# Shorter GpSimd sums, a later place for c's second half, and another order in the first and last pair of a two-layer gated network kernel

## The chip, the cores and the metric

One core of one Trainium2 chip. The metric is the device time of one execution in microseconds, as the median of several runs. TensorE is called PE in the profile, VectorE DVE, ScalarE ACT, GpSimd POOL and SyncE SP; PEld is TensorE's weight load, which overlaps the matmuls.

## The reference, cut to what matters

```python
x = x + L0_ffn(L0_cond(x, slot), ...)      # conditioned: x @ W + b + 2 (x @ A[slot]) @ B[slot]
x = x + L1_ffn(L1_cond(x, lang), ...)      # both linear, each with routed adapters (top 2 of 8)

# L0_ffn: y = (silu(c @ Wg.T) * (c @ Wu.T)) @ Wd.T            512 -> 1376 -> 512
# L1_cond: c = x @ W.T + 2 * sum_e gate[e] * (x @ A[e]) @ B[e]
# L1_ffn: y = c @ W2.T + b + 2 * sum_e combine[e] * (c @ A2[e]) @ B2[e]
```

x has 128 x 32 = 4096 tokens of 512 features, all in float32. The gates of the second layer are a softmax over the two best of eight experts.

## The kernel before, in words

**Tiles.** The tokens lie along the columns: 8 tiles of 512 tokens (NT = 8), each of four blocks of 128 features (KC = 4), 128 x 512 elements a block. Two tiles form a pair, a *stage* s of the middle part and a pair u of the last part (NS = 4).

**Precision.** Every float32 operand is split in two: `hi`, a copy rounded to TensorE's float32r made by ScalarE, and `lo`, the difference, made by VectorE. Three matmuls (hi hi, hi lo, lo hi) stand for one product; `mm3`, which calls `mm` at L1813, issues them. So behind each operand stand a ScalarE instruction, a VectorE instruction and a TensorE wait for the second.

**Seven products.** The large products are done on 2 x 2 blocks with seven block products instead of eight (numbered 1 to 7, order `ORDER = [1, 7, 6, 2, 5, 4, 3]`). They need sums of the operands: t1 to t4 of the token side, s1 to s4 of the weight side. Four banks (a, y, w, z) take the products; ScalarE copies a bank into the next one where two results share a product (`begin_y`, `begin_z`), and VectorE adds the seventh product, kept in a scratch tile, to two of them (`sum_c21`, `sum_c22`, and v).

**Order of the program.** First the conditioning layer for 8 tiles, whose result c is stored to memory. Then, for each of the four stages: gate and up products (slots "g", 11 blocks of 128 hidden columns with seven products each), with `silu` on ScalarE and the products h on VectorE (L1481, L1488), and the down products (slots "d", 35 steps). Weights come through a ring of 12 tiles that SyncE fills in the order in which TensorE uses them; its other transfers stand in that same queue (`extras`). Last comes a stage of folded weights (the two linear layers of L1 are multiplied together, `weight_product`, five of them) and four pairs u = 0 to 3, each of two blocks (mp = 0, 1), with routers.

**Around the change.** Each engine runs its own program in order; semaphores tie them. Nothing is scheduled at run time, so the place of a call in `act_program`, `dve_program` or `pe_program` is its place in the queue.

- *Pair sums* (`pair_sums`, L834 to L855): GpSimd forms t3, t1, t2 and t4 of a stage's result, four operations on 128 x 1024 elements, and counts them in `pair_sum_done`. For stages 0 to 2 they run in the next stage's second gate block; SyncE stores them (`store_sums`) behind weight loads. For stage 3 they run at the start of the last stage, and ScalarE's `route_x(0)` and `copy_7_l` wait for them. The four sums over the folded weights (L922 to L928) follow on GpSimd.
- *c's operands* (`COP_BEHIND`, L520): during the down steps of stage s the fourteen operands of c for stage s + 1 are split, each behind a chosen down step n. The first seven are of c's first half, the other seven of its second. `cop_begin` forms two differences on VectorE when c has landed; `load_c(s + 1, 1)` on SyncE waits for the seventh split. `op_split` and `op_rest` are the ScalarE and VectorE halves of down operand n; a down operand needs the place of operand n - 8, so TensorE's slot of that one. `down_z22` (the v of the down product, L1498) runs behind n = 32, and TensorE's `down_single(s, 0)` waits for it.
- *Weight products*: `weight_product(i)` on TensorE fills a right and a left bank; ScalarE copies them, VectorE makes the low parts (L1567 right, L1570 left) and so frees them. `route_x(0)` on TensorE, four groups c of 12 matmuls, takes for its first group the right bank of product 3, then the left one of 3, then right and left of 4.
- *A pair of the last stage*: the programs at L1311 to L1365 (ScalarE), L1770 to L1807 (VectorE) and L2094 to L2128 (TensorE). `router(i, t)` is a chain of 11 to 14 small VectorE operations for tile t (i = 0: first adapter, i = 1: second) with one exponential on ScalarE in it. `turn_h(i, t)` transposes the routed tile on TensorE, copies it on ScalarE and makes its low part on VectorE (L1647), which the products `out_h1` and `out_h2` need. `route_h(t)` feeds the first adapter's result to the second router. `split_t(u, i)` splits a stored sum t_i (L1529). In a block, TensorE's product 7 waits for `gc22_done` of the block before (VectorE, `sum_c22_l`, L1546) and for the split of t3:

```python
if i == 7:
    ...
        e.wait_ge(gc22_done, gate_turn(n - 1))
...
    t = {7: 3, 6: 2, 5: 1, 4: 4}[i]
    e.wait_ge(t_lo_done, t_split(u, t))
```

  Products 4 and 5 wait for `yz_done`, ScalarE's `begin_z_l` (L1271), which is behind product 6 of the block.

## Time and profile before

| | |
|---|---|
| median of 3 runs | 1000.36 us (999.42 to 1001.5) |
| the profiled execution | 1001.15 us |
| its span in the profile | 999.4 us |
| mean granted TensorE clock | 0.998 |
| instructions | 13989 |

The span runs from the first to the last instruction of the profile; the time of the same execution is 1.75 us longer. In the rows of a group, the names are written output <- inputs, the shape is partitions x elements, "idle before" is the time for which the engine did nothing ahead of the instructions, and the arrow names what ended it. A timeline row gives the start and the duration in us; several like instructions in a row are merged (x2). Matmuls are pipelined: their durations overlap, and one of 512 columns starts 0.227 us after the other.

### The profile page before, as it was taken

How to read it: one execution, taken by the hardware profiler on the slowest of the kernel's cores; microseconds unless marked ns; L12 is line 12 of the kernel's file. 1: busy time of each engine (PE TensorE's matmuls, PEld its weight loads, DVE VectorE, ACT ScalarE, POOL GpSimd, SP SyncE). 2: the span in 40 equal slices, each digit the busy share in tenths (PEclk: the TensorE clock that was granted, in tenths of full speed). 3: DMA queues.
4: the chain of work that ended last, by engine and by line, in shares of the span. 5: the costliest groups of instructions: out<-in, count | busy, mean ns of one | idle time of the engine just before them, and what ended most of it. 6: DMA issues, size and time to landing. Idle time of an engine off the chain costs nothing.

```text
span 999.4 us, 13989 instructions
## 1 busy us (share of the span) xinstructions
PE 983.9 (98%) x4787; PEld 829.5 (83%) x4787; DVE 599.5 (60%) x969; ACT 464.5 (46%) x854; POOL 244.6 (24%) x192
## 2 busy tenths in 40 slices
PE   8999999999999999999999999999999998999998
PEld 7888888888878788888888887888888988888876
DVE  5644596776983632685533497342376587585762
ACT  5635566555742333571333373333356363535342
POOL 5232332654300621400513220341141520000000
PEclk9999999999999999999999999999999999999999
DMA  8997866676968876877887767986687730615122
GB/s 282 358 324 287 307 220 245 216 267 234 336 230 293 269 208 191 281 243 252 276 265 193 239 225 251 324 274 198 191 307 281 261 122 22 232 45 209 66 104 85
DMA packets 121485, 230.11 MB, mean 230 GB/s; under 512 B 12612, under 2 KB 12612, under 8 KB 121160
## 3 DMA queue, kind: packets, MB, share of 16 engines
q1 hardware_dynamic: 118880, 220.81, 65.9%
q0 software_dynamic: 2400, 8.41, 2.3%
q8 instruction: 39, 0.64, 0.3%
q14 instruction: 30, 0.25, 0.1%
q10 hardware_dynamic: 136, 0.01, 0.0%
HBM read 165.74 MB, written 63.44 MB: 229 GB/s over the span
## 4 chain that ended last, share of the span: by engine, by line
PE 79%; DVE 14%; issue 2%; DMA 2%; ACT 1%; SPq 0%; DVEq 0%; ACTq 0%
PE bank L1813 78%; DVE op_lo L1452 5%; DVE cop_lo L1438 2%; DMA c<-c_scratch 2%; PE bank L1837 1%; DVE h_lo L1457 1%; ACT xs_hi L1120 1%; PE bank L1974 1%; DVE h L1488 1%; DVE s L1488 1%; DVE xs_lo L1523 0%; DMA slot_i<-in_slots 0%; DVE c L1432 0%; DVE c L1443 0%; DVE c_t L1430 0%
## 5 line engine op out<-in xcount | busy, mean ns | idle before, releaser
L1813 PE MATMUL bank<-cop_hi,wring 128*128 128x512 f32 x1234 | 381.1, 389 | 0.7 <-DVE v L1466 0.7
L1813 PEld LDWEIGHTS bank<-cop_hi,wring 128*128 128x128 f32 x1234 | 231.6, 188 | 50.0 <-DVE v L1466 1.6
L1813 PE MATMUL bank<-cop_lo,wring 128*128 128x512 f32 x616 | 239.7, 389 | 0.0
L1813 PE MATMUL bank<-op_hi,wring 128*128 128x512 f32 x560 | 174.6, 390 | 1.9 <-DVE op_lo L1452 1.9
L1466 DVE TENSOR_TENSOR v<-bank,p7s 128x512 f32<-128x512 f32 x44 | 30.4, 691 | 191.1 <-PE bank L1813 191.0
L1813 PEld LDWEIGHTS bank<-cop_lo,wring 128*128 128x128 f32 x616 | 115.6, 188 | 23.7
L1813 PEld LDWEIGHTS bank<-op_hi,wring 128*128 128x128 f32 x560 | 105.1, 188 | 25.1 <-issue 3.1
L1813 PE MATMUL bank<-op_lo,wring 128*128 128x512 f32 x280 | 109.0, 389 | 0.0
L1066 ACT ACTIVATE s<-bank 128x512 f32<-128x512 f32 x44 | 26.3, 598 | 117.9 <-PE bank L1813 117.8
L1452 DVE TENSOR_TENSOR op_lo<-h,op_hi 128x512 fp32r<-128x512 f32 x100 | 77.7, 794 | 3.8 <-ACT op_hi L1023 3.6
L1023 ACT ACTIVATE op_hi<-h 128x512 fp32r<-128x512 f32 x100 | 62.3, 626 | 13.4 <-PE bank L1813 12.6
L820 POOL TENSOR_TENSOR h_t<-h,h 128x512 f32<-128x512 f32 x20 | 26.6, 1328 | 170.3 <-DVE h L1488 170.3
L1035 ACT ACTIVATE bank<-bank 128x512 f32<-128x512 f32 x44 | 25.6, 582 | 77.5 <-PE bank L1813 77.5
L1813 PEld LDWEIGHTS bank<-op_lo,wring 128*128 128x128 f32 x280 | 52.6, 188 | 10.8
L1813 PE MATMUL bank<-xa_hi,w_hi 128*128 128x512 f32 x128 | 50.8, 397 | 1.2 <-DVE w_lo L1383 1.2
L850 POOL TENSOR_TENSOR t_sum<-x_second,x_second 128x1024 f32<-128x1024 f32 x3 | 7.2, 2401 | 179.8 <-DMA x_second<-x_scratch 179.8
L1813 PE MATMUL bank<-xa_lo,w_hi 128*128 128x512 f32 x128 | 50.0, 391 | 0.0
L1813 PE MATMUL bank<-xa_hi,w_lo 128*128 128x512 f32 x128 | 49.9, 390 | 0.0
L1471 DVE TENSOR_TENSOR p7s<-bank,p7s 128x512 f32<-128x512 f32 x44 | 30.4, 691 | 23.9 <-PE bank L1813 23.7
L1057 ACT ACTIVATE s<-bank 128x512 f32<-128x512 f32 x44 | 26.3, 598 | 30.6 <-PE bank L1813 30.6
L1042 ACT ACTIVATE p7s<-bank 128x512 f32<-128x512 f32 x44 | 26.3, 598 | 30.4 <-PE bank L1813 30.4
L1488 DVE TENSOR_TENSOR h<-s,v 128x512 f32<-128x512 f32 x40 | 34.9, 874 | 8.2 <-ACT s L1066 8.0
(228 smaller groups left out, 1916.1 us busy)
## 6 DMA issues: line engine op xcount, KB each, us to landing
wring<-wgu_scratch SPq DMA_DIRECT2D x231, 256.0 KB, 2.9
wring<-wd_scratch SPq DMA_DIRECT2D x140, 256.0 KB, 5.3
wgu_scratch<-wring SPq DMA_DIRECT2D x77, 256.0 KB, 3.6
x_raw<-in_x SPq DMA_DIRECT2D x32, 256.0 KB, 7.5
c_scratch<-c_out SPq DMA_DIRECT2D x32, 256.0 KB, 2.8
c<-c_scratch SPq DMA_DIRECT2D x32, 256.0 KB, 4.4
xs_raw<-x_scratch SPq DMA_DIRECT2D x16, 512.0 KB, 6.9
out<-res SPq DMA_DIRECT2D x32, 256.0 KB, 2.1
```

The source lines that it names most:

```text
L820: e.tensor_tensor(h_t3[p][:, :], h22[p][:, :], h12[p][:, :], ALU.subtract).then_inc(t3_done, 1)
L1023: e.activation(op_hi[n % N_OP][:, :], op_source[i][p][:, :], ACT.Copy).then_inc(op_hi_done, 1)
L1035: e.activation(bank_y[b][:, :], bank_a[b][:, :], ACT.Copy).then_inc(ay_done, 1)
L1042: e.activation(p7s[b][:, :], bank_w[b][:, :], ACT.Copy).then_inc(p7s_done, 1)
L1057: e.activation(s1[j % 2][:, :], bank_a[j % 2][:, :], ACT.Silu).then_inc(silu1_done, 1)
L1066: e.activation(s2[j % 2][:, :], bank_z[j % 2][:, :], ACT.Silu).then_inc(silu2_done, 1)
L1438: e.tensor_tensor(cop_lo[i][:, q, :], cop_source[i][:, :], plain(cop_hi[i][:, q, :]), ALU.subtract).then_inc(cop_lo_done, 1)
L1452: e.tensor_tensor(op_lo[n % N_OP][:, :], op_source[i][p][:, :], plain(op_hi[n % N_OP][:, :]), ALU.subtract).then_inc(op_lo_done, 1)
L1466: e.tensor_tensor(v[b][:, :], bank_z[b][:, :], p7s[b][:, :], ALU.add).then_inc(gc22_done, 1)
L1471: e.tensor_tensor(p7s[b][:, :], bank_y[b][:, :], p7s[b][:, :], ALU.add).then_inc(gc21_done, 1)
L1488: e.tensor_tensor(dst[:, :], s2[b][:, :], v[b][:, :], ALU.mult).then_inc(h2_done, 1)
L1813: return e.matmul(out_ap, lhs, rhs, start=start, stop=stop, skip_group_check=True)
```

## The change

It does four things. `PIECES = 4`: each of the four pair sums is made in four operations of 128 x 256 elements (two halves k, two column ranges h) instead of one of 128 x 1024, each counts in `pair_sum_done`, and all waits for that semaphore are multiplied; each of the four waits for all pieces of the one before (t2 had no such wait before). The four sums over the folded weights are made in two operations each, of 128 x 256. In `COP_BEHIND` the eighth operand of c (the first of its second half) stands behind down step 27 instead of 25, and the following ones move up so that the thirteenth stands behind step 32, called behind `down_z22`, instead of step 31. `weight_product(3)` is called before `split_t(0, 3)`, on ScalarE and VectorE. And in the pairs: the first pair's `router(0, 2)` comes behind the sums of the first block instead of before the transposed tiles; of the router tiles' copies on ScalarE one instead of two stands before an exponential; in the third pair (u = 2, the last that prepares another) `split_t(3, 3)` and `split_t(3, 2)` come before `router(1, 6)`, and `turn_h(0, 7)` behind the block's sums.

```diff
--- before.py
+++ after.py
@@ -467,6 +467,7 @@
         return 4 * u + t_order(u).index(i) + 1
 
     S_SPLITS = [3, 1, 2, 4]
+    PIECES = 4
 
     def l_place(u, i):
 
@@ -517,7 +518,7 @@
         return rhs2_sb[:, i, :], rhs2_hi[:, i, :], rhs2_lo[:, i, :]
 
 
-    COP_BEHIND = dict(zip((11, 13, 14, 15, 16, 19, 20, 25, 27, 28, 29, 30, 31, 33), range(len(cop_order))))
+    COP_BEHIND = dict(zip((11, 13, 14, 15, 16, 19, 20, 27, 28, 29, 30, 31, 32, 33), range(len(cop_order))))
 
 
 
@@ -605,7 +606,7 @@
                     else:
                         e.wait_ge(x2_stored["c11", mp], DMA * s)
                         e.wait_ge(x2_stored["c21", mp], DMA * s)
-                        e.wait_ge(pair_sum_done, 4 * s)
+                        e.wait_ge(pair_sum_done, PIECES * 4 * s)
                     e.dma_start(res[mp][:, :], x[2 * s, mp]).then_inc(res_in[mp], DMA)
                     e.dma_start(res[2 + mp][:, :], x[2 * s, 2 + mp]).then_inc(res_in[2 + mp], DMA)
             if pos == slot_at["d", 1, 1] and s == NS - 1:
@@ -657,7 +658,7 @@
 
         def store_sums(s):
             for n, (i, tile) in enumerate(((3, t3_sum), (1, x2_second[0]), (2, t2_sum), (4, x2_second[1]))):
-                e.wait_ge(pair_sum_done, 4 * s + n + 1)
+                e.wait_ge(pair_sum_done, PIECES * (4 * s + n + 1))
                 e.dma_start(t_dram[s, i - 1].rearrange("k p f -> p k f"), tile[:, :, :]).then_inc(t_stored, DMA)
 
         def load_x2(u, j, h):
@@ -670,7 +671,7 @@
                 e.wait_ge(pe_slot, NS * N_SLOT)
                 for mp in range(2):
                     e.wait_ge(x2_stored["c12", mp], DMA * NS)
-                e.wait_ge(pair_sum_done, 4 * NS - 2)
+                e.wait_ge(pair_sum_done, PIECES * (4 * NS - 2))
             else:
                 e.wait_ge(pe_acc, l_mark(u - 2, 1, {(0, 0): 1, (0, 1): 5, (1, 0): 5, (1, 1): 3}[j, h]))
             e.dma_start(xs_raw[u % 2][j][:, 2 * h:2 * h + 2, :],
@@ -847,12 +848,17 @@
                 e.wait_ge(cop_lo_done, 14 * NS)
             else:
                 e.wait_ge(x2_second_in, 2 * DMA * (s + 1))
-            e.tensor_tensor(t3_sum[:, :, :], b22[:, :, :], b12[:, :, :], ALU.subtract).then_inc(pair_sum_done, 1)
-            e.wait_ge(pair_sum_done, n + 1)
-            e.tensor_tensor(t1[:, :, :], b12[:, :, :], b11[:, :, :], ALU.subtract).then_inc(pair_sum_done, 1)
-            e.tensor_tensor(t2_sum[:, :, :], t3_sum[:, :, :], b11[:, :, :], ALU.add).then_inc(pair_sum_done, 1)
-            e.wait_ge(pair_sum_done, n + 3)
-            e.tensor_tensor(t4[:, :, :], b21[:, :, :], t2_sum[:, :, :], ALU.subtract).then_inc(pair_sum_done, 1)
+
+            for done, (out_, in0, in1, op) in enumerate((
+                    (t3_sum, b22, b12, ALU.subtract), (t1, b12, b11, ALU.subtract),
+                    (t2_sum, t3_sum, b11, ALU.add), (t4, b21, t2_sum, ALU.subtract))):
+                if done > 0:
+                    e.wait_ge(pair_sum_done, PIECES * (n + done))
+                for k in range(2):
+                    for h in range(PIECES // 2):
+                        cols = slice(h * 2 * TOK // PIECES, (h + 1) * 2 * TOK // PIECES)
+                        e.tensor_tensor(out_[:, k, cols], in0[:, k, cols], in1[:, k, cols],
+                                        op).then_inc(pair_sum_done, 1)
 
         e.iota(part_i[:, :], [[0, 1]], base=0, channel_multiplier=1).then_inc(pool_const, 1)
         e.memset(ident[:, :], 0.0).then_inc(pool_const, 1)
@@ -918,14 +924,14 @@
         pair_sums(NS - 1)
         a11, a21 = m2_raw[:, 0:2, 0:2 * P], m2_raw[:, 0:2, 2 * P:]
         a12, a22 = m2_raw[:, 2:4, 0:2 * P], m2_raw[:, 2:4, 2 * P:]
-        e.wait_ge(m2_raw_done, 4)
-        e.tensor_tensor(s_raw[3][:, :, :], a11, a21, ALU.subtract).then_inc(s_sum_done, 1)
-        e.wait_ge(m2_raw_done, 2 * KC)
-        e.tensor_tensor(s_raw[1][:, :, :], a21, a22, ALU.add).then_inc(s_sum_done, 1)
-        e.wait_ge(s_sum_done, 2)
-        e.tensor_tensor(s_raw[2][:, :, :], s_raw[1][:, :, :], a11, ALU.subtract).then_inc(s_sum_done, 1)
-        e.wait_ge(s_sum_done, 3)
-        e.tensor_tensor(s_raw[4][:, :, :], a12, s_raw[2][:, :, :], ALU.subtract).then_inc(s_sum_done, 1)
+        for done, (i, in0, in1, op) in enumerate((
+                (3, a11, a21, ALU.subtract), (1, a21, a22, ALU.add), (2, s_raw[1], a11, ALU.subtract),
+                (4, a12, s_raw[2], ALU.subtract))):
+            e.wait_ge(m2_raw_done, 4 if i == 3 else 2 * KC)
+            if done > 1:
+                e.wait_ge(s_sum_done, 2 * done)
+            for k in range(2):
+                e.tensor_tensor(s_raw[i][:, k, :], in0[:, k, :], in1[:, k, :], op).then_inc(s_sum_done, 1)
 
 
 
@@ -1125,13 +1131,13 @@
             e.activation(hi, first, ACT.Copy).then_inc(t_hi_done, 1)
 
         def split_s(i):
-            e.wait_ge(s_sum_done, S_SPLITS.index(i) + 1)
+            e.wait_ge(s_sum_done, 2 * (S_SPLITS.index(i) + 1))
             e.wait_ge(pe_ring, ring_full("left", KC, 0))
             e.activation(s_hi[i][:, :, :], s_raw[i][:, :, :], ACT.Copy).then_inc(fold_hi_done, 1)
 
         def route_x(t, cs=range(TC)):
             if t == 0:
-                e.wait_ge(pair_sum_done, 4 * NS)
+                e.wait_ge(pair_sum_done, PIECES * 4 * NS)
                 for mp in range(2):
                     e.wait_ge(x2_stored["c12", mp], DMA * NS)
                     e.wait_ge(x2_stored["c22", mp], DMA * NS)
@@ -1252,7 +1258,7 @@
             n = l_turn(u, mp)
             e.wait_ge(pe_acc, l_mark(u, mp, 7))
             if n == 0:
-                e.wait_ge(pair_sum_done, 4 * NS)
+                e.wait_ge(pair_sum_done, PIECES * 4 * NS)
                 for half in range(2):
                     e.wait_ge(x2_stored["c11", half], DMA * NS)
                     e.wait_ge(x2_stored["c21", half], DMA * NS)
@@ -1294,8 +1300,8 @@
         split_x2(0, 1, 0)
         weight_product(2)
         split_x2(0, 1, 1)
+        weight_product(3)
         split_t(0, 3)
-        weight_product(3)
         split_t(0, 2)
         weight_product(4)
         split_t(0, 4)
@@ -1334,17 +1340,17 @@
                 route_x(a + 2, (0, 1))
                 router(1, a if u == 0 else b)
                 route_x(a + 2, (2, 3))
-                route_x(b + 2, (0, 1))
+                route_x(b + 2, (0,))
                 router(*((1, b) if u == 0 else (0, a + 2)))
-                route_x(b + 2, (2, 3))
-                if u == 0:
-                    router(0, a + 2)
+                route_x(b + 2, (1, 2, 3))
             else:
                 router(1, b)
             turn_h(1, a)
             turn_h(1, b)
             close_l(u, 0, "c11")
             close_l(u, 0, "c12")
+            if u == 0:
+                router(0, a + 2)
             begin_y_l(u, 1)
             copy_7_l(u, 1)
             if more:
@@ -1747,8 +1753,8 @@
         split_x2(0, 1, 0)
         weight_product(2)
         split_x2(0, 1, 1)
+        weight_product(3)
         split_t(0, 3)
-        weight_product(3)
         split_t(0, 2)
         weight_product(4)
         split_t(0, 4)
@@ -1779,29 +1785,30 @@
                 split_x2(u + 1, 1, 0)
                 split_x2(u + 1, 1, 1)
             router(1, b)
-            if more:
+            if more and u > 0:
                 router(0, a + 2)
             turn_h(1, a)
             turn_h(1, b)
             sum_c21_l(u, 0)
             sum_c22_l(u, 0)
             if more:
+                if u == 0:
+                    router(0, a + 2)
                 router(0, b + 2)
                 turn_h(0, a + 2)
                 route_h(a + 2)
+                split_t(u + 1, 3)
+                split_t(u + 1, 2)
                 if u + 2 < NS:
-                    split_t(u + 1, 3)
-                    split_t(u + 1, 2)
                     split_t(u + 1, 1)
+                    turn_h(0, b + 2)
                 else:
                     router(1, a + 2)
-                turn_h(0, b + 2)
             sum_c21_l(u, 1)
             sum_c22_l(u, 1)
             if more:
                 if u + 2 == NS:
-                    split_t(u + 1, 3)
-                    split_t(u + 1, 2)
+                    turn_h(0, b + 2)
                     split_t(u + 1, 1)
                 split_t(u + 1, 4)
                 route_h(b + 2)
```

## Rows read from the trace of the kernel before

**Rows 1.** The page, part 1: busy time and share of each engine.

```profile
PE 983.9 (98%) x4787; PEld 829.5 (83%) x4787; DVE 599.5 (60%) x969; ACT 464.5 (46%) x854; POOL 244.6 (24%) x192
```

**Rows 2.** TensorE's waits: who waited <- whom, us in total, times, longest.

```profile
PE bank L1813 <- DVE hg_lo L1647: 3.3, 1, 3.3
PE bank L1813 <- DVE op_lo L1452: 1.9, 3, 0.9
PE bank L1813 <- issue: 1.8, 1, 1.8
...
PE bank L1813 <- DVE m_lo L1567: 0.8, 1, 0.8
PE bank L1813 <- DVE v L1466: 0.7, 2, 0.5
PE bank L1813 <- DVE v L1498: 0.6, 3, 0.2
```

**Rows 3.** Timeline, VectorE and GpSimd, 320 to 336: start, us, instruction, [idle before].

```profile
326.23 2.90 DVE L1481 TENSOR_TENSOR h<-s,p7s 128x512 f32<-128x512 f32 x1
...
328.55 2.84 POOL L853 TENSOR_TENSOR t_sum<-t_sum,res 128x1024 f32<-128x1024 f32 x1
```

**Rows 4.** GpSimd's groups: by line (busy, mean ns), and min/median/max ns.

```profile
L850 POOL TENSOR_TENSOR t_sum<-x_second,x_second 128x1024 f32<-128x1024 f32 x3 | 7.2, 2401 | 179.8 <-DMA x_second<-x_scratch 179.8
...
L791 POOL TENSOR_TENSOR gs<-wg_raw,wu_raw x11: 736/740/1245, 121.6 to 230.6; 128x256 f32<-128x256 f32 x11
```

**Rows 5.** Timeline of SyncE's queue, 336 to 342: the fourth store of sums.

```profile
339.77 1.27 SPq L661 DMA_DIRECT2D t_scratch<-x_second  x1
```

**Rows 6.** Timeline, TensorE 287 to 290 and VectorE 280 to 300.

```profile
288.00 0.39 PE L1813 MATMUL bank<-op_hi,wring 128*128 128x512 f32 x1
289.30 0.47 PE L1813 MATMUL bank<-op_hi,wring 128*128 128x512 f32 x1 [0.92 <-DVE op_lo L1452]
...
285.74 0.69 DVE L1430 TENSOR_TENSOR c_t<-c,c 128x512 f32<-128x512 f32 x1 [4.24 <-DMA c<-c_scratch]
...
296.49 1.28 DVE L1498 TENSOR_TENSOR v<-bank,v 128x512 f32<-128x512 f32 x2
```

**Rows 7.** Timeline of VectorE, 799 to 806, at the folded weights.

```profile
799.79 2.30 DVE L1529 TENSOR_TENSOR t_lo<-t_raw,t_hi 128x1024 fp32r<-128x1024 f32 x1
...
803.09 0.28 DVE L1567 TENSOR_TENSOR m_lo<-bank,m_hi 128x128 fp32r<-128x128 f32 x1
```

**Rows 8.** Last stage, first and second pair: timeline; last row a window with PEclk.

```profile
842.26 0.19 DVE L1584 SCALAR_TENSOR_TENSOR logit<-lang_hot,lx 128x32 f32<-128x32 f32 x1
846.44 1.29 DVE L1647 TENSOR_TENSOR hg_lo<-bank,hg_hi 128x512 fp32r<-128x512 f32 x2
...
843.38 0.60 PE L1974 MATMUL bank<-ident,hg 128*128 128x128 f32 x4
...
851.61 0.48 PE L1813 MATMUL bank<-xs_hi,m_hi 128*128 128x512 f32 x1
...
894.80 0.60 PE L1974 MATMUL bank<-ident,hg 128*128 128x128 f32 x4
...
898.30 0.40 PE L1813 MATMUL bank<-xs_hi,m_hi 128*128 128x512 f32 x1
...
898.86 0.19 DVE L1595 TENSOR_TENSOR diff<-logit,top 128x32 f32<-128x32 f32 x1
...
856.00 0.58 ACT L1271 ACTIVATE bank<-bank 128x512 f32<-128x512 f32 x1 [0.55 <-PE bank L1813]
...
849.00:850.00 1.00, 1.00 (x4) 0.76 (x3) 0.69 (x1) 0.00 (x0) 0.00 (x0) 0.50 0.18 70
```

**Rows 9.** Timeline of VectorE, 956 to 968, at the last pair.

```profile
957.89 0.19 DVE L1591 TENSOR_REDUCE top<-lx 128x4 f32<-128x32 f32 x1
...
962.94 0.69 DVE L1647 TENSOR_TENSOR hg_lo<-bank,hg_hi 128x512 fp32r<-128x512 f32 x1
...
964.75 2.35 DVE L1529 TENSOR_TENSOR t_lo<-t_raw,t_hi 128x1024 fp32r<-128x1024 f32 x2
```

## The prediction

> **What bounds the kernel now.** I read the page first, then TensorE's waits, then the timeline around each wait. The page shows TensorE busy for 98% of the span [rows 1], so the matmuls are the bound, and an edit on another engine pays only where TensorE waits. The list of TensorE's waits [rows 2] is the whole purse: 3.3 us for one half of a transposed adapter tile, 1.9 in three waits for `op_lo`, 1.8 that it calls "issue", 0.8 for a half of the folded weights, 0.7 in two waits for v of the gate and 0.6 in three for v of the down product. The idle time understates a gap, since a matmul is drawn 0.39 long while they start every 0.227 us: between the two matmuls of [rows 6] lie 1.30 us, so the `op_lo` gap of 0.92 cost 1.07, and the first matmul after it ran 0.08 long (0.47 against 0.39). I add 0.25 us to each listed wait.
>
> **Pair sums in pieces, stages 0 to 2.** The product h of VectorE, both inputs in SBUF, takes 2.90 us while GpSimd adds [rows 3], against 0.69 for such an operation undisturbed [rows 6]. The next two VectorE operations have the same length, and behind them waits v, which TensorE wants. The row of GpSimd beside it, 2.84 against 2.40 undisturbed [rows 4], shows that the engines take turns by whole instructions, also where GpSimd's next instruction has no semaphore wait ahead of it (L852 to L853). A piece of 256 columns takes 0.74 [rows 4]. So each of the three VectorE operations waits at most 0.74 instead of 2.2; VectorE gains over 4 us, and v is late by only 0.5 and 0.2. Both waits go: 0.7 + 2 x 0.25 = **1.2 us**. The price: sixteen pieces are 11.8 us against 4 x 2.4 = 9.6, and with three or four VectorE turns of 0.6 to 0.7 they end about 14 us after their start at 323.7, near 338. SyncE issues the fourth store at 339.8 [rows 5], and its queue of weight loads runs twelve slots ahead of TensorE, so its wait for the count 16 holds nothing up. Bounds: 0.7 to 1.3.
> By the Trainium skill's "GPSIMD Engine Reference", section 3.1, 2048 elements take 4497 ns, which would make a piece 0.56 us and the cut free. By that the sums would end 2.8 us sooner and nothing in the forecast would change, as the fourth store has the time either way; the row of 0.74 says otherwise and is what I use.
>
> **Second half of c two operands later.** VectorE waits for c from step 25, until 285.74 [rows 6]; `op_lo` 26 stands behind the wait, and TensorE stops. After the change steps 26 and 27 are split before it: their ScalarE halves need TensorE slots 18 and 19, which end near 278.7 and 280.1 (slots of 6 x 0.227 = 1.36 us, counted back from 288.2), so they are done by 282. Next due is `op_lo` 28, at 288.2 + 2 x 1.36 = 290.9: c's two differences, one split, one difference and the split of 28 are five operations of 0.6 to 0.7 from 285.74, ready at 289.2. Step 29: ready 291.3, due 292.3. The second wait of the stage is for v of the down product, ready at 297.8 [rows 6]. Three operations of 0.6 (splits 26 and 27, and c's twelfth split, which now comes after v) leave the queue before it: 296.0, due 288.2 + 4 x 1.36 + 2.72 = 296.4. All six waits of three stages go: 1.9 + 0.6 + 6 x 0.25 = 4.0, measured start to start 3.9; I take **3.9**. The slack of 0.4 for v is thin, so the bounds are 2.4 and 4.0. No DMA is moved: c's load is gated by the seventh split of the first half, whose place is unchanged.
>
> **Folded weights (start of the last stage).** VectorE's split of t takes 2.30 us (1.15 of it waiting for GpSimd) ahead of the fourth weight product, whose half is free at 803.4 [rows 7]; TensorE has then been idle for 0.8, since 802.6. Now the weight product goes first: it starts at about 799.8 instead of 802.0, and its half is free near 801.2. That wait of 0.8 + 0.25 goes. But two splits of t now stand together ahead of the fifth weight product: fourth done 802.0, then ScalarE and VectorE for the two splits, 2.7, and 0.2: 804.9 undisturbed, with GpSimd's pieces in between (0.3 and 0.7) 805.9. TensorE wants that bank at 802.5 + 3.0 = 805.5. I expect a new wait of about 0.3 there: net **0.8**, bounds -0.3 and 1.05. The sums over the folded weights are earlier by the fourth product's two us; they have no waiter now. GpSimd's pair sums end near 800 instead of 798.8, and their first waiter, ScalarE's copy of the router tiles, has until about 807.
>
> **First pair of the last stage.** VectorE runs a router, 842.26 to 846.44, ahead of the adapter tile that TensorE wants, and ScalarE has the router's exponential ahead of the same tile. Afterwards TensorE ran at a granted clock of 0.50 [rows 8], 1.2 GHz. From the transposes to the next block's first matmul pass 851.61 - 843.38 = 8.23 us; in the second pair, where no router stands there, 898.30 - 894.80 = 3.50. With the router behind the block's sums both pairs have the same order: **4.7 us**, slow clock included. What is late next: two routers now follow the sums. By the second pair's row the first one's difference ends 0.75 us after the block starts [rows 8], the second's 4.18 later, at 4.93; ScalarE's exponential stands before the copy that starts bank z (exponential 0.14 to the next start, copy 0.58), so the copy ends at 5.7. TensorE wants it after four products, 4 x 1.36 = 5.44. So a new wait of 0.3, with its start 0.4: net **4.3**, bounds 3.3 and 4.75. The moved copies of router tiles (one ahead of an exponential, not two) let the second router run about 1 us earlier, which nobody waits for.
>
> **Last pair.** The "issue" wait is for product 7, which needs two things: the split of t3, done at 965.9 (the first half of the row of 964.75), and the previous block's v sum, done at 964.8, because it gives bank w free. Today the order is router (957.89 to 962.94), tile, two sums, splits [rows 9]. The change puts two splits first (2.26 us from 957.8), then the router (5.05), then the sums (0.6 + 0.68): the splits are ready at 960.1, but the v sum only at 957.8 + 2.26 + 5.05 + 1.28 = 966.4. Product 7 then starts 0.5 later than today. ScalarE's exponential comes 2.3 later with the router, and the tile copies queued behind it delay TensorE by less than that, ahead of the same wait. **-0.5 us**, bounds -0.8 and 0.
>
> **Sum.** 1.2 + 3.9 + 0.8 + 4.3 - 0.5 = 9.7 us. The profiled execution took 1001.15 us for a span of 999.4 (1.75 around it), so it would take 991.4. It is 0.8 above the median of the runs, 1000.36: **990.7 us** there. About 0.2%, 2 us, is what a measurement of this kernel can tell from no change.
>
> **Rivals.**
> (a) The last pair pays: if the split were the only thing product 7 waits for, the 1.8 + 0.25 would go instead of 0.5 coming: 988.1. For it: the release came 0.1 after the split and 1.2 after the sum. Against it: the program's wait for the sum. 6%.
> (b) GpSimd keeps the port through pieces that have no semaphore wait between them. Four pieces then block VectorE as one instruction did, 3.0 us: the 1.2 and the 0.8 are lost, 992.7. Against it: VectorE got its turn between L852 and L853. The rule behind it is the Trainium skill's "SBUF — State Buffer", section "Who interferes with whom", by which issue order decides who blocks. 6%.
> (c) The thin slacks break: c lands later than 285.5 after its issue, or the two routers in a row delay the second pair's tiles too. Half of 3.9 and 2 us more are lost: 994.6. Against it: VectorE is busy for only 60% of the span [rows 1], and its work in that block has not grown. 9%.
> (d) Slower: each piece pays for the port. The pair sums of the last stage start at 786.55 and ScalarE's router copies wait for them; TensorE needs the first by 808.5. At p us a piece, TensorE stops for 16p - 21.5, and the waits of the first and third terms stay (2.0). It is slower than before from 16p = 29.2, p = 1.8. At 2.4, the longest piece of [rows 4], 1.245, plus a VectorE split of 1.15 every time, it would be 990.7 + 2.0 + 16.9 = 1009.6. The longest of the eleven speaks for it, their median of 0.74 and VectorE's few operations in that stretch against. 2%.
> (e) The edits change nothing at c's operands, because c is the limit whatever stands behind it: 994.6 as well. 4%, since the operations behind the wait are named.
> The forecast has the remaining 73%, its own range 989.2 to 992.6. The range over all, 988.3 to 994.0, takes in (a), (b) and the bounds of the terms; it leaves out (d), most of (c) and (e). Faster by over 0.2%: 95%, all but (d) and a sum of lower bounds; within: 3%; slower: 2%.
>
> **What would show it.** In TensorE's waits: no `op_lo`, no v of either kind, no `hg_lo` of 3.3, no slow clock near 845; short new ones behind a copy to bank z in the first pair (0.1 to 0.3 idle), and behind `m_lo` (0 to 0.5); a wait of about 1.9 in the last pair, now released by the sum of L1546's line. VectorE's h product beside the sums at 1.4 or less, GpSimd's pieces at 0.74. A saving under 6 us, or a last pair without a wait, would prove a step wrong.

## The result, and the profile after

The kernel before was run beside each set, on the same chip.

| | time, us (median) | ratio to before |
|---|---|---|
| before, beside the first set | 999.89 | |
| after, first set | 994.2 (992.9 to 994.35) | 0.9939, 95% [0.9922, 0.9957] |
| before, beside the second set | 1001.21 | |
| after, second set | 992.97 (991.5 to 993.54) | 0.9923, [0.9908, 0.9938] |
| forecast | 990.7 (988.3 to 994.0) | |

It is faster, as forecast, by 5.7 us in the first set and 8.2 in the second instead of 9.7, and the first median lies 0.2 above the range. The profiled execution took 994.31 us for a span of 992.6.

The page of after, part 1:

```profile
PE 982.7 (99%) x4787; PEld 830.4 (84%) x4787; DVE 586.8 (59%) x969; ACT 464.9 (47%) x854; POOL 256.0 (26%) x244
```

GpSimd is busy for 11.4 us more [rows 1]. VectorE is busy for 12.7 less, since the time for which an operation is blocked counts as busy and it no longer stands behind whole sums in stages 0 to 2. TensorE's waits of after:

```profile
PE bank L1820 <- DVE res L1552: 1.9, 1, 1.9
PE bank L1820 <- DVE warm L1663: 1.5, 1, 1.5
PE bank L1820 <- ACT bank L1041: 0.9, 1, 0.9
PE bank L1820 <- DVE w_lo L1389: 0.8, 1, 0.8
PE bank L1820 <- issue: 0.8, 1, 0.8
PE bank L1820 <- ACT res L1285: 0.3, 2, 0.2
PE bank L1820 <- ACT bank L1277: 0.2, 1, 0.2
```

Of the waits of before [rows 2] that the sum counted, `hg_lo` (3.3), `op_lo`, both v and `m_lo` are gone. The 1.9 for `res` and the 0.2 for ScalarE's bank were foretold; the 0.8 called "issue" was not, and it stands elsewhere than the old one. The timelines of VectorE and GpSimd beside the pair sums:

```profile
327.20 0.94 DVE L1487 TENSOR_TENSOR h<-s,p7s 128x512 f32<-128x512 f32 x1
328.06 1.22 DVE L1458 TENSOR_TENSOR op_lo<-h,op_hi 128x512 fp32r<-128x512 f32 x1
329.21 1.22 DVE L1494 TENSOR_TENSOR h<-s,v 128x512 f32<-128x512 f32 x1
...
324.76 2.83 POOL L860 TENSOR_TENSOR t_sum<-x_second,x_second 128x256 f32<-128x256 f32 x4 [59.18 <-DMA x_second<-x_scratch]
327.67 4.05 POOL L860 TENSOR_TENSOR x_second<-x_second,res 128x256 f32<-128x256 f32 x4
```

The three VectorE operations take 0.94 to 1.22 instead of 2.9 [rows 3]; the second sum takes 4.05 in four pieces, because VectorE has its turns between them. The last stage of after, timelines of TensorE, VectorE, GpSimd and ScalarE:

```profile
820.01 0.47 PE L1820 MATMUL bank<-xs_hi,s_hi 128*128 128x512 f32 x1 [0.78 <-issue]
...
806.83 0.72 DVE L1590 SCALAR_TENSOR_TENSOR logit<-lang_hot,lx 128x32 f32<-128x32 f32 x1
...
810.51 0.19 DVE L1630 SCALAR_TENSOR_TENSOR picked<-rank,expo 128x32 f32<-128x32 f32 x1 [0.32 <-ACT expo L1156]
...
818.68 1.23 DVE L1535 TENSOR_TENSOR xs_lo<-xs_raw,xs_hi 128x1024 fp32r<-128x1024 f32 x1
...
806.50 1.70 POOL L934 TENSOR_TENSOR s_raw<-m_raw,s_raw 128x256 f32<-128x256 f32 x2
...
808.23 0.63 ACT L1136 ACTIVATE s_hi<-s_raw 128x512 fp32r<-128x512 f32 x1 [1.21 <-POOL s_raw L934]
810.18 0.23 ACT L1156 ACTIVATE expo<-diff 128x32 f32<-128x32 f32 x1
...
849.15 0.58 ACT L1277 ACTIVATE bank<-bank 128x512 f32<-128x512 f32 x1
849.78 0.50 PE L1820 MATMUL bank<-xs_hi,s_hi 128*128 128x512 f32 x1 [0.17 <-ACT bank L1277]
...
958.46 0.68 DVE L1552 TENSOR_TENSOR res<-bank,res 128x512 f32<-128x512 f32 x1
959.19 0.50 PE L1820 MATMUL bank<-t_hi,s_hi 128*128 128x512 f32 x1 [1.93 <-DVE res L1552]
```

Read from below: product 7 of the last pair starts 0.05 after the v sum, which now comes behind splits and router. Product 5 of the first pair's second block waits for ScalarE's copy, whose predecessor is an exponential. And product 5 of the very first block waits until 820.01 for VectorE's low half of t1 (its tile bears the name `xs_lo`), done at 819.91. VectorE is late because two routers stand ahead of that split, and the first of them is late. Its exponential (810.18) stands on ScalarE behind the split of s4, which waits for GpSimd's last sum over the folded weights (ends at 808.20).

The exponential is only one of two ways in which these sums reach VectorE. Before, the same router began its chain of small operations 5.4 us ahead of the first block, and the first of them took 0.18:

```profile
810.28 0.18 DVE L1584 SCALAR_TENSOR_TENSOR logit<-lang_hot,lx 128x32 f32<-128x32 f32 x1
...
812.59 0.23 ACT L1150 ACTIVATE expo<-diff 128x32 f32<-128x32 f32 x1
```

After, it begins 4.9 ahead of the block; that first operation takes 0.72 beside GpSimd's running pieces, and the chain up to the use of the exponential 0.8 more than before. Then VectorE stands idle for 0.32 until the exponential is there. Of the 1.5 us by which this router ends later against the block, 0.5 are the later start, 0.8 the slower operations and 0.2 the exponential. By an estimate from the same rows, the exponential alone would have held the router up for nearly as long, since it starts 1.6 ahead of the block instead of 3.1.

Where the 6.8 us between the spans are, start to start between the same matmuls in both traces:

| stretch | before | after | difference | forecast |
|---|---|---|---|---|
| start of the span to the first gate block | 147.63 | 149.09 | +1.5 | 0 |
| stages 0 to 3 | 637.09 | 632.72 | -4.4 | -5.1 |
| folded weights to the first h1 product | 55.46 | 55.44 | 0.0 | -0.8 |
| to the first pair's second block | 11.43 | 6.77 | -4.7 | -4.7 |
| to the last pair | 93.30 | 93.62 | +0.3 | +0.4 |
| the last pair and the end | 54.51 | 54.95 | +0.4 | +0.5 |

Two of the losses lie outside what the change touches. Timelines of TensorE after, in the opening and in stage 0:

```profile
7.12 0.63 PE L1820 MATMUL bank<-xa_lo,w_hi 128*128 128x512 f32 x1
7.55 0.63 PE L1820 MATMUL bank<-xa_hi,w_lo 128*128 128x512 f32 x1
...
210.48 0.50 PE L1820 MATMUL bank<-cop_hi,wring 128*128 128x512 f32 x1 [0.87 <-ACT bank L1041]
```

The first matmuls start 0.43 apart, not 0.227, for some 3.5 us (1.7 lost); the wait at 210 cost 1.03. Without it stages 0 to 3 gained 5.4.

### The profile page after: what moved, and what is told of

Its sections match the earlier page's. It is cut to its first block, busy times and chain, and to the rows that moved or that the text cites. A ratio compares the mean times of both kernels' runs of the same rounds, so it can differ in the third digit from the quotient of the medians.

```text
span 992.6 us, 14042 instructions
## 1 busy us (share of the span) xinstructions
PE 982.7 (99%) x4787; PEld 830.4 (84%) x4787; DVE 586.8 (59%) x969; ACT 464.9 (47%) x854; POOL 256.0 (26%) x244
## 4 chain that ended last, share of the span: by engine, by line
PE 96%; DVE 1%; ACT 1%; issue 1%; DMA 0%; SPq 0%; ACTq 0%; DVEq 0%
PE bank L1820 95%; PE bank L1844 1%; PE bank L1981 1%; DMA w_raw<-in_w 0%; ACT xs_hi L1126 0%; ACT bank L1277 0%; DVE hg L1644 0%; DVE t_lo L1535 0%; DVE greater L1624 0%; ACT res L1285 0%; DVE diff L1601 0%; DVE top L1597 0%; DVE wins L1620 0%; DVE rank L1627 0%; DVE greater L1618 0%
## 5 line engine op out<-in xcount | busy, mean ns | idle before, releaser
L1458 DVE TENSOR_TENSOR op_lo<-h,op_hi 128x512 fp32r<-128x512 f32 x100 | 72.9, 747 | 3.3 <-ACT op_hi L1029 3.1
L1029 ACT ACTIVATE op_hi<-h 128x512 fp32r<-128x512 f32 x100 | 62.7, 627 | 13.6 <-PE bank L1820 12.7
L860 POOL TENSOR_TENSOR t_sum<-x_second,x_second 128x256 f32<-128x256 f32 x12 | 8.9, 780 | 177.3 <-DMA x_second<-x_scratch 177.3
L776 POOL DMA_INDIRECT ab<-in_ab_table,row_i x16 | 18.7, 1171 | 81.9 <-DVE b_lo L1400 75.8
```

The costliest lines, as they stand in the source:

```text
L776: e.indirect_dma_start(out=ab[g][:, :], out_offset=None, in_=ab_table, in_offset=bass.IndirectOffsetOnAxis(ap=row_i[:, col:col + 1], axis= ...
L1029: e.activation(op_hi[n % N_OP][:, :], op_source[i][p][:, :], ACT.Copy).then_inc(op_hi_done, 1)
L1458: e.tensor_tensor(op_lo[n % N_OP][:, :], op_source[i][p][:, :], plain(op_hi[n % N_OP][:, :]), ALU.subtract).then_inc(op_lo_done, 1)
```

## Experiments

Each is the changed kernel with the edit shown, unless it says otherwise. Traces are compared start to start, since the 95% intervals of the medians are +/- 1.2 us at best and 2.4 at worst. "Theory A" and "theory B" are those of the expectation that stands with the run.

**1. The changed kernel again.** 

> The changed kernel once more. Theory A (the parts gave what the walk through the queues says, about 9.0 us, and the missing 2.6 us of the profiled execution are chance delays in code that the change leaves alone: a granted clock of 0.5 in the first 4 us and one late load of gate weights near 210): the profile has neither or only one of the two, its span is 990 to 991.5, and the waits from 240 on are the same to 0.2 us. Theory B (the change itself slows the opening, by its place in memory or by its longer programs): both delays stand there again at the same size, span 992.6.

992.97 us, ratio 0.9923; in its trace the wait at 210 is gone and the opening takes 6.1 instead of 7.3; span 990.2, 9.2 below before. All waits from 240 on are the same. So the two losses were chance, and the change is worth 8 us by this set (7.7 by the ratio).

**2. c's operands as before.**

```diff
-    COP_BEHIND = dict(zip((11, ..., 20, 27, 28, 29, 30, 31, 32, 33), ...
+    COP_BEHIND = dict(zip((11, ..., 20, 25, 27, 28, 29, 30, 31, 33), ...
```

> Only the place of c's second half is put back to step 25. Theory A: the waits for op_lo and for the v of the down product come back in stages 0 to 2, 3.9 us start to start, so 3.9 us slower than the changed kernel. Theory B (c's landing was the limit either way): the time of the changed kernel within 1 us.

996.09 us, 0.9952 [0.9937, 0.9966]: 3.1 slower than run 1. Its waits on TensorE, and when VectorE got c in the first and third stage:

```profile
PE bank L1820 <- DVE op_lo L1458: 0.5, 1, 0.5
...
PE bank L1820 <- DVE v L1504: 0.2, 1, 0.2
...
285.38 0.69 DVE L1436 TENSOR_TENSOR c_t<-c,c 128x512 f32<-128x512 f32 x1 [2.58 <-DMA c<-c_scratch]
602.13 0.69 DVE L1436 TENSOR_TENSOR c_t<-c,c 128x512 f32<-128x512 f32 x1 [3.81 <-DMA c<-c_scratch]
```

Only the third stage waits. From the first of c's DMA issues to VectorE's start pass 5.6, 5.5 and 6.8 us in the three stages, against 7.2, 6.5 and 7.1 in the execution that the forecast was worked out from. The lost time follows c's landing, and that execution had three late ones. Over the 14 traces it runs from 5.5 to 7.5.

Start to start, this trace loses 1.2 us to the undone edit (1.0 of it at the two waits), not 3.1. Of the rest of its 3.8 against run 1's, 1.1 lie in the opening and 1.6 behind a fall of the granted clock in the last pair. So the trace bears out theory A's mechanism, and its 3.9 only for an execution in which c lands late.

**3. The first pair's router back ahead of the tiles** (ScalarE and VectorE).

```diff
-            if more and u > 0:
+            if more:
                 router(0, a + 2)
```

> Only the router's place in the first pair is put back (the copies of the router tiles stay as changed). Theory A: TensorE's wait of about 3 us in front of out_h2 comes back with the slow clock behind it, and the new wait of 0.3 for the copy to bank z goes: 4.2 us slower than the changed kernel. Theory B (the slow clock would have come anyway or costs nothing): 3 us or less.

997.11 us, 0.9957 [0.9943, 0.9971], 4.1 slower than run 1. TensorE's wait, and a window behind it (busy times, then PEclk, DMA share, GB/s):

```profile
PE bank L1818 <- DVE hg_lo L1653: 2.3, 1, 2.3
...
845.00:847.00 2.00, 2.00 (x8) 1.57 (x8) 1.24 (x2) 0.00 (x0) 0.00 (x0) 0.75 0.35 132
```

The stretch to the second block is 10.56 against 6.77, so 3.8 us longer; the wait at bank z is gone (0.4), which makes 3.4 net against the 4.2 of theory A, and the granted clock falls again. The old wait was a microsecond longer [rows 2]. Here the router starts 2.1 us ahead of the transposes instead of 1.1; the moved copies of router tiles, still in place, may be why, which no run separates.

**4. The third pair's order as before** (splits behind the sums, the tile ahead).

```diff
                 route_h(a + 2)
-                split_t(u + 1, 3)
-                split_t(u + 1, 2)
...
+                    split_t(u + 1, 3)
+                    split_t(u + 1, 2)
                     split_t(u + 1, 1)
```

> Only the third pair's order is put back. Theory A (product 7 is released by the sum of v in the changed kernel, 0.4 to 0.5 later than by the split in the order before): 0.4 us faster than the changed kernel, the wait of 1.9 at product 7 shrinks to 1.8 and the longer transposes before it vanish. Theory B (the new order is a gain hidden by noise): 1 us or more slower than the changed kernel.

993.99 us, 0.9932 [0.9915, 0.995], within the noise of run 1. Product 7 starts after 1.82 idle, and the block starts 0.3 earlier against its neighbour (17.79 against 18.07): the new order costs 0.4. The time can't show it: the median lies 1.0 above run 1's, the other way.

**5. The folded-weight sums whole.**

```diff
-            for k in range(2):
-                e.tensor_tensor(s_raw[i][:, k, :], in0[:, k, :], in1[:, k, :], op).then_inc(s_sum_done, 1)
+            e.tensor_tensor(s_raw[i][:, :, :], in0[:, :, :], in1[:, :, :], op).then_inc(s_sum_done, 1)
```

> The changed kernel with the four sums over the folded weights whole again (four operations of 128x512), the sixteen pieces of the pair sums kept. In question is TensorE's new wait of 0.78 idle (0.94 start to start) for product 5 of the last stage's first block, at 817 to 820, behind VectorE's split of t1. Theory A: the pieces of these sums finish later, ScalarE's split of s4 and with it its exponential of the first router stand behind them, and the router's VectorE chain pushes the split of t1: with whole sums the last one ends 0.5 to 1.5 earlier, the exponential starts that much earlier and the wait at product 5 falls under 0.3; 0.5 to 1.0 us faster than the changed kernel (ratio to before about 0.9915 to 0.992). No old wait of 0.8 for the half of the folded weights returns (its order was the cause). Theory B: the pieces of the pair sums, which start these sums 2.6 later, or the two splits of t in a row are the cause: the wait stays at 0.6 to 1.0, time as the changed kernel, 0.9923.

995.42 us, 0.9951 [0.9934, 0.9969]. The wait at product 5 is gone, as theory A had it, but another took its place, at the fifth weight product, where the forecast had put one of 0.3; neither theory foresaw it. A TensorE wait, the cause on VectorE, and a window in the last pair:

```profile
PE bank L1819 <- DVE m_lo L1572: 0.8, 1, 0.8
...
799.35 4.07 DVE L1534 TENSOR_TENSOR t_lo<-t_raw,t_hi 128x1024 fp32r<-128x1024 f32 x2 [0.38 <-ACT t_hi L1130]
...
960.00:962.00 2.00, 2.00 (x6) 1.56 (x5) 2.00 (x2) 0.01 (x1) 0.00 (x0) 0.50 0.81 302
```

Two splits that took 2.97 in run 1 take 4.07 beside whole sums, and the half of the folded weights behind them is late. The stretch of the folded weights is 55.5, as with pieces (55.4). Of its other time, 1.5 us went where the granted clock fell to 0.50 after the wait of the last pair, which run 1 had without that fall, and 1.6 in the opening.

**6. All sums whole** (`PIECES = 1` too). 

> The changed kernel with all of GpSimd's sums whole again (PIECES = 1 and the sums over the folded weights whole), the three other edits kept. Theory A: in each of stages 0 to 2 VectorE's operations beside the pair sums take 2.9 again and waits for v of the gate return, 0.7 idle in all, 1.2 start to start; in the last stage GpSimd starts the sums over the folded weights 2.6 earlier, the wait at product 5 of the first block vanishes (0.94 back), so that the pieces as a whole are worth only 0.3: time within 0.5 us of the changed kernel. Theory B: the wait at product 5 is a matter of the order on VectorE and ScalarE and stays: 1.2 us slower than the changed kernel (ratio 0.9935).

992.78 us, 0.9933 [0.9909, 0.9957], within the noise of run 1. VectorE and GpSimd in stage 1:

```profile
325.71 1.06 DVE L1482 TENSOR_TENSOR h<-s,p7s 128x512 f32<-128x512 f32 x1
326.69 2.88 DVE L1453 TENSOR_TENSOR op_lo<-h,op_hi 128x512 fp32r<-128x512 f32 x1
329.50 2.88 DVE L1489 TENSOR_TENSOR h<-s,v 128x512 f32<-128x512 f32 x1
...
326.30 2.73 POOL L857 TENSOR_TENSOR x_second<-x_second,res 128x1024 f32<-128x1024 f32 x1
```

Here h comes at 325.71, while GpSimd is still in its first sum (it ends at 326.22), and waits for the rest of that one; the two behind it take 2.88 each. Together 6.8, against 8.7 before, where h came 0.03 after the second sum had begun [rows 3]. v is in time or nearly so: stages 1 to 3 lose 0.2 us together. In the last stage a wait of 0.3 for `m_lo` is left and none at product 5: 55.0 against 55.4. Neither theory had this: the waits for v do not return, and beside the other edits the pieces as a whole are worth nothing (0.2 gained in the stages, 0.4 lost in the last one).

**7. `weight_product(3)` behind `split_t(0, 3)` again.** 

> The changed kernel with the third weight product's calls behind split_t(0, 3) again, on ScalarE and VectorE. Theory A: the old wait of 0.7 to 1.0 for a half of the folded weights returns near 800, and since VectorE's work behind it is the same, the wait at product 5 of the first block is shorter by about what was lost ahead of it, 0 to 0.3 left: time within 0.4 us of the changed kernel, so this edit is worth nothing net, not 0.8. Theory B, the prediction's: the edit is worth 0.8, the old wait returns in full and the wait at product 5 stays: 0.8 to 1.0 slower (ratio 0.993).

993.18 us, 0.9936 [0.9917, 0.9954]. The old wait returns only in small (0.3 start to start), the wait at product 5 is 0.50 instead of 0.78, and the stretch is 55.5 against 55.4. The edit is worth nothing net, as theory A had it, though that expected the old wait back at 0.7 to 1.0. Start to start, the old wait was 1.0 with whole sums and the old order (before and in run 10), and it is 0.3 and 0.2 with the old order and pieces (here and in run 11). So the pieces alone take most of it. The new order alone takes it too, but then a wait of 0.3 stands at the fifth weight product (run 6).

**8. Another order in the third pair.** On VectorE the tile, t1 and the two sums ahead of the router, and ScalarE likewise:

```diff
                 else:
-                    router(1, a + 2)
+                    turn_h(0, b + 2)
+                    split_t(u + 1, 1)
             sum_c21_l(u, 1)
             sum_c22_l(u, 1)
             if more:
                 if u + 2 == NS:
-                    turn_h(0, b + 2)
-                    split_t(u + 1, 1)
+                    router(1, a + 2)
```

> The changed kernel with another order in the third pair only: on VectorE the splits of t3 and t2, the tile of the second routed block, the split of t1 and the two sums of the second block stand ahead of router(1, 6), which stood ahead of the sums; ScalarE's router exponential goes behind the two copies out of the banks. Theory A: product 7 of the last pair waits for the v sum alone (1.93 idle, 2.1 start to start); the sum then ends about 3 earlier, before TensorE gets there, and nothing takes its place: 2.0 to 2.3 us faster than the changed kernel, ratio to before 0.990 to 0.9903. Theory B: the router's later end delays the second layer's routed tiles of the last pair (the adapter tile of its first block), and a wait of 1 to 3 appears behind it: same or slower than the changed kernel.

990.49 us, 0.9909 [0.9888, 0.9929], 2.5 below run 1 (1.4 by the ratios); from the first pair's second block to the end the trace is 2.5 shorter. The v sum and product 7:

```profile
953.81 0.68 DVE L1555 TENSOR_TENSOR res<-bank,res 128x512 f32<-128x512 f32 x1
...
955.51 0.39 PE L1823 MATMUL bank<-t_hi,s_hi 128*128 128x512 f32 x1
```

The sum is done a microsecond before TensorE gets there, and no wait takes its place. Theory A.

**9. The last stage's pair sums whole, all other sums in pieces.**

```diff
+                if last:
+                    e.tensor_tensor(out_[:, :, :], in0[:, :, :], in1[:, :, :], op).then_inc(pair_sum_done, 1)
+                    continue
                 for k in range(2):
```

> The changed kernel with the pair sums of the last stage alone whole again (four operations of 128x1024); those of stages 0 to 2 and the sums over the folded weights stay in pieces. Known so far, from the start of the folded weights to the first h1 product of the last stage (start to start): both kinds in pieces 55.4 with a wait of 0.78 at product 5, only the folded-weight sums whole 55.5 with a wait of 0.76 for a half of the folded weights instead, both whole 55.0 with one of 0.31. Theory A (queue on GpSimd): whole pair sums end about 2 earlier, the folded-weight sums behind them too, ScalarE's split of s4 and its exponential start 1.5 to 2 earlier and the wait at product 5 goes; VectorE's t splits meet only pieces of 0.74, so the wait for the half of the folded weights stays away: 54.4 to 54.6, 0.9 faster than the changed kernel (ratio 0.9914). Theory B (the port): whatever GpSimd runs beside VectorE's two t splits blocks them, whole pair sums for up to 2 us: a wait of 0.3 to 0.8 for the folded weights appears, 55.0 or more, no gain over the changed kernel (0.9923).

VectorE and ScalarE ahead of the first block, which starts at 810.54:

```profile
805.12 0.19 DVE L1596 SCALAR_TENSOR_TENSOR logit<-lang_hot,lx 128x32 f32<-128x32 f32 x1
...
807.44 0.23 ACT L1162 ACTIVATE expo<-diff 128x32 f32<-128x32 f32 x1
```

The exponential starts 3.1 ahead of the block, as before; with all pieces it was 1.6. The router's first operation starts 5.4 ahead and takes 0.19, also as before. Of TensorE's waits both the one at product 5 and the one for `m_lo` are gone, and the stretch is 54.5: theory A in the trace. It shows the cause of the new wait, GpSimd's late sums; how much of it came through the exponential and how much through VectorE's blocked operations it doesn't separate. The time, 993.49 us, 0.9935 [0.9911, 0.9959], can't show a gain of 0.9: this trace reaches the first gate block 1.0 later than run 1's.

**10. The kernel before, with only c's second half later.** 

> The kernel before with one edit alone: c's second half two operands later. Its own six waits go (start to start 3.9 by the trace of before; undoing it in the changed kernel cost 3.1). In question is what happens to the waits for v of the gate beside the pair sums, whose 0.7 idle (two of three stages, 1.2 start to start) my forecast gave to the pieces. With every edit but the pieces there was none of them left. Theory A: how long VectorE's h product is blocked depends on how far GpSimd is in its second sum when it comes (1.60 after the first sum's start and later: h took 1.7 to 2.2 and v was in time; 0.4 to 0.6 after: 2.7 to 2.9 and v was late), and without the stalls of the down products the sums start 0.5 to 0.7 earlier against TensorE; so this edit alone takes most of the v waits too: 0 to 0.2 idle left, stages 1 to 3 at 157.8 to 157.9 each, 4.3 to 5.1 us faster than before (ratio 0.995 to 0.9957). Theory B: only the pieces take them away: v waits of 0.4 to 0.5 in two stages stay, 3.1 to 3.9 faster (0.9961 to 0.9969).

998.24 us, 0.998 [0.9965, 0.9996], a gain of 2.1 us, less than either theory; its trace has a span of 996.2 with the fall of the clock in the last pair (1.6). GpSimd and VectorE in stage 1:

```profile
324.55 2.40 POOL L852 TENSOR_TENSOR x_second<-x_second,res 128x1024 f32<-128x1024 f32 x1
...
325.06 2.44 DVE L1481 TENSOR_TENSOR h<-s,p7s 128x512 f32<-128x512 f32 x1
```

h comes half a microsecond into the second sum instead of at its very start. No v wait of either kind is listed any more; start to start the two of the gate have shrunk from 1.3 us to 0.4. The stages 1 and 2 take 158.06 and 157.91 where before took 159.44 and 159.82, and a stage without any stall 157.76. Theory A in the trace: this edit alone takes most of the gate's v waits too, and stages 0 to 3 are 4.2 shorter than in the trace of before, in which c landed late.

**11. The kernel before, with only the pieces.** 

> The kernel before with the first edit alone, complete: all pair sums in pieces of 256 columns and the folded-weight sums in two pieces each; c's operands and all orders as before. With the other three edits in place the pieces were worth 0.2 in stages 0 to 2 and cost 0.4 in the last one (the run with all sums whole against the changed kernel, from the traces). Theory A (the edits overlap): here, where the stalls of the down products make the sums start late against VectorE, the pieces take both waits for v of the gate, 1.2 start to start, and leave the six of c's operands; in the last stage they delay ScalarE's exponential and give back 0.4 to 1.0 as a wait at product 5: net 0.2 to 0.8 faster than before, ratio 0.999 to 1.0, that is nothing that can be measured. Theory B, the forecast's: 1.2 faster with nothing given back (0.9988).

999.06 us, 0.9986 [0.9973, 0.9998]. Its TensorE waits in the stages:

```profile
PE bank L1819 <- DVE v L1504: 0.6, 3, 0.2
...
PE bank L1819 <- DVE op_lo L1458: 0.4, 2, 0.2
```

The v waits of the gate are gone, and those of the down product stand as before. `op_lo` has shrunk too (1.9 before), which neither theory had, but not by the pieces. Three traces have c's old order: before, run 2 and this one. In their nine stages the loss at `op_lo`, start to start, is c's time from issue to VectorE less 6.15 us, or nothing, with pieces or without:

| c landed after | 7.2 | 7.1 | 6.8 | 6.6 | 6.5 | 6.5 | 6.2 | 5.6 | 5.5 |
|---|---|---|---|---|---|---|---|---|---|
| trace | before | before | run 2 | run 11 | run 11 | before | run 11 | run 2 | run 2 |
| lost at `op_lo` | 1.1 | 1.0 | 0.6 | 0.4 | 0.4 | 0.3 | 0.1 | 0 | 0 |

Stages 1 and 2 give the overlap, 319.26 before: c's edit alone saves 3.3, the pieces alone 2.2, both 3.7, down to twice 157.76, and there is no more to gain. Of the 2.2, 0.8 is c's earlier landing in this trace, which leaves 1.3 to the pieces. So the two edits share about 0.9, and it is the part of the gate's v waits that run 10 lost without any pieces.

**12. What the runs point to, together:** runs 8 and 9, and in the first pair ScalarE's copy ahead of the second router's exponential.

```diff
-            if more:
+            if more and u > 0:
                 router(0, b + 2)
             begin_z_l(u, 1)
+            if u == 0:
+                router(0, b + 2)
```

> The changed kernel with what the runs point to, together: whole pair sums in the last stage alone, the sums of the third pair ahead of router(1, 6) (2.2 to 2.4 in its own run), and in the first pair ScalarE's copy that starts bank z ahead of router(0, 3)'s exponential (the wait of 0.16 idle, 0.43 start to start, at 847). If they add up: 2.3 + 0.9 + 0.4 = 3.6 us faster than the changed kernel, 989.4, ratio to before 0.9888, and of the waits in the last stage only the two of 0.15 for ScalarE's res and the first stage's are left. If the gain of the folded weights' part doesn't show (theory B of last_sums_whole): 990.3, ratio 0.9897. Against it: the exponential, later by up to 1.5, makes router(0, 3) late, and the transposes of the second pair's first block wait for it: not faster than the run with the third pair's order alone, 0.9909.

989.51 us (988.9 to 990.39), 0.9892 [0.9874, 0.9911], in spite of a slow opening in its trace. All TensorE waits that are left:

```profile
PE bank L1831 <- DVE warm L1674: 1.5, 1, 1.5
PE bank L1831 <- DVE w_lo L1400: 0.5, 1, 0.5
PE bank L1831 <- ACT res L1291: 0.3, 2, 0.2
```

The first two stand at the very start. It is 10.8 us faster than before and 3.5 below run 1 (3.1 by the ratios), where 3.6 was expected. The edits add up (the trace is 2.5 shorter than run 1's with an opening 1.2 longer), and this version beats both kernels.

## Why the forecast was right or wrong, point by point

- **Direction, and what there was to gain.** Right. TensorE's waits were all there was to gain, and each wait that was to go went, though not each by the edit that was to take it. The forecast's own sign of a wrong step, "a saving under 6 us", did show in the first set (5.7 by the medians, 6.1 by the ratio).
- **First pair, 4.3.** Right in size and parts: 4.67 gross, and a new wait of 0.43 start to start at bank z, released by the copy behind the exponential. Undoing it cost 3.4 net in the trace, 4.1 by the medians; the moved copies stayed.
- **Last pair, -0.5.** Right: `res` releases product 7 after 1.93, 0.4 to 0.5 lost. Rival (a) is out, since product 7 did wait for the sum; the mistake was the kernel's, and the sums ahead of the router bring 2.5.
- **Pair sums 1.2 and c's operands 3.9.** Together right in this trace (5.4 against 5.1), because all these waits went. Two steps failed. The 1.2 was booked to the pieces, while the same stalls at c's operands decide when GpSimd's sums meet VectorE's h: c's edit alone takes most of the gate's v waits (run 10), and beside it the pieces are worth 0.2 to 0.5 (runs 6 and 10 against stages without a stall). The other way round there is nothing of the kind: the pieces leave c's waits alone (run 11). And "measured start to start 3.9" was one execution's, with c landing after 7.2, 6.5 and 7.1 us; in the other traces it mostly came sooner, and undoing the edit cost 1.2 in the trace and 3.1 by the medians. The lower bound of 2.4 covered the new order's risk, not that the old order loses less in other executions. That, with the chance losses below, is why the medians moved by 5.7 and 8.2 us and the spans by 6.8 and 9.2. How much each explains is not settled: the intervals are too wide.
- **Folded weights, 0.8.** Wrong: 0.0. The old wait went, for which the pieces alone nearly suffice (run 7), and none came at the fifth weight product. The step that failed is the sentence that the sums over the folded weights "have no waiter now". Relative to the first block they ended 2.9 us later (before, GpSimd had stood idle for 2.29 among them), ScalarE's split of s4 waited for them with an exponential behind it, VectorE's router ran beside them and was blocked, and so the split of t1 came late. Run 9 shows that GpSimd's queue is the cause: with it shorter, the wait is gone, and the folded weights take 0.9 us less than before, where the forecast had 0.8.
- **Rivals (b), (d).** Not seen. VectorE got its turn between pieces with no semaphore wait between them, and the pieces' price was 14.8 us for the last stage's pair sums against 12.2, 0.16 a piece. That cost the 0.9 above and is nothing like 1.8 a piece. The Trainium skill's "SBUF — State Buffer", section "Who interferes with whom", lets issue order decide who blocks; the trace agrees only in that a running piece is waited for, and the next one in the queue is not.
- **Rivals (c), (e).** Not seen, although (c)'s time, 994.6, is near the first median: the waits that it needs are not in the trace. In run 12 c landed 7.5 us after its issue in one stage, and that stage took 157.86, 0.1 more than the undisturbed 157.76.
- **The range.** It was said to take in rival (a), but (a)'s 988.1 lies below its end of 988.3. One median lies above 994.0 and the other below it, so on which side the time fell was a matter of the chance losses.

## What to carry to other kernels

Two edits that remove stalls of the same engine in the same loop are not to be added before asking whether the stalls set each other's phase: here 3.3 and 1.3 made 3.7. And to learn what one of them did, look at where each wait went in a run with that edit alone. Work whose result was early is not without a waiter. Name who waits for it on every other engine, and what stands behind that wait in the same queue (here an exponential in the middle of a chain); name also who runs beside it and is slowed by it. And where a wait is for a DMA, take its price from several executions or from several loop turns with the landing times beside it, not from the sum of one trace.

## What was not expected of the hardware

- TensorE's first matmuls started 0.43 us apart for some 3.5 us in 7 of the 14 traces and mostly 0.227 apart in the others, the changed kernel's own two traces being one of each; the stretch up to the first transposes takes 7.1 to 7.5 instead of 5.5 to 6.1. The column of the granted clock showed it (0.50, 1.2 GHz) in only one of the seven and read 1.00 in the rest.
- After the same wait of 1.8 to 1.9 us in the last pair, the granted clock fell to 0.50 in 5 of 12 traces, for about 3 us, which costs 1.5 to 1.6; in the two traces without the wait it stayed at 1.00. The granted clocks of all executions fit: in run 1, three with a mean granted clock of 1.0 took 991.5 to 992.6 us and three with 0.998 took 993.4 to 993.5, and none of the nine of runs 8 and 12, which lack that wait, has less than 0.999. Where in these executions the clock fell isn't recorded. Two versions without the wait are little proof, but they point to a second gain from removing it, the loss by chance.
- c's load took from 5.5 to 7.5 us from its first issue to VectorE's start, in the same place of the same program.
